# Up projection of an attention and feed-forward block: bias rows in two bands of 32 partitions, both halves of a tile issued together

## The reference, cut to what matters

```
q, k, v = split(x @ Wqkv.T + bqkv)            # 16 heads of 16
q, k = elu(q*scale) + 1, elu(k*scale) + 1
y = q * cumsum(k*v) / max(sum_d(q * cumsum(k)), 1e-3)
x = layernorm(x + y @ Wproj.T + bproj)
h = gelu(quant(x) @ quant(w_fc).T + b_fc)      # 256 -> 1024: the up projection
x = layernorm(x + quant(h) @ quant(w_proj).T + b_proj)   # 1024 -> 256: the down projection
```

## Time and profile before

| | us |
|---|---|
| median of 3 runs | 276.52 |
| lowest, highest | 276.45, 277.63 |
| span of the profiled execution, first to last instruction | 273.3 |
| busy: PE, DVE, POOL, ACT | 240.0, 238.9, 155.0, 151.0 |
| one middle stage, from one `mean_var_1` to the next | 29.6 |
| mean granted clock of TensorE, as a share of 2.4 GHz | 0.982 |

### The profile page before, as it was taken

How to read it: one execution, slowest core, us unless ns; L and a number is a source line. 1 busy time by engine, 2 the same in 40 slices (tenths; PEclk the granted TensorE clock), 3 DMA queues, 4 the chain that set the end, 5 groups by cost and what they waited for, 6 DMA issues and landing times.

```text
span 273.3 us, 3668 instructions
## 1 busy us (share of the span) xinstructions
PE 240.0 (88%) x1204; PEld 143.4 (52%) x1204; DVE 238.9 (87%) x513; ACT 151.0 (55%) x246; POOL 155.0 (57%) x118
## 2 busy tenths in 40 slices
PE   7999889997999899989999899989999989838761
PEld 7546636653566446644656356644664455524340
DVE  1398997998998999899989999899989997978962
ACT  2663277745556851855475754685285646332823
POOL 1076466575376656476566737675647656655851
PEclk9999999999999999999999999999999997979997
DMA  6940020036202473227304490238224530642022
GB/s 155 365 97 2 0 78 1 2 70 155 46 0 38 77 193 42 38 39 190 81 0 77 114 160 0 41 64 205 38 36 44 110 83 0 65 90 78 0 79 77
DMA packets 49474, 20.70 MB, mean 76 GB/s; under 512 B 38960, under 2 KB 49200, under 8 KB 49456
## 3 DMA queue, kind: packets, MB, share of 16 engines
q1 hardware_dynamic: 47824, 20.20, 32.7%
q10 hardware_dynamic: 1632, 0.27, 0.6%
HBM read 7.35 MB, written 4.19 MB: 42 GB/s over the span
## 4 chain that ended last, share of the span: by engine, by line
DVE 56%; PE 25%; DMA 8%; POOL 4%; issue 3%; ACT 2%; SPq 1%; ACTq 0%; POOLq 0%; DVEq 0%
DVE vbank L857 12%; PE abank L1116 8%; DVE hq L758 7%; DVE vbank L821 6%; PE dbank L1193 5%; DVE kvsum L799 4%; DMA h<-in_L_ffn_w_fc_dram 4%; POOL h_round L380 3%; PE hbank L1184 3%; DVE r L815 3%; DVE r L869 3%; DVE vbank L834 3%; DMA xqT<-xq 2%; DVE h_pow L750 2%; DVE kf L782 2%
## 5 line engine op out<-in xcount | busy, mean ns | idle before, releaser
L1116 PE MATMUL abank<-xT,WqkvT 128*128 128x512 f32 x176 | 81.6, 599 | 3.6 <-DVE kf L782 2.2
L380 POOL TENSOR_TENSOR h_round<-h,h_inv 128x1024 f16<-128x1024 f32 x32 | 66.5, 2079 | 31.2 <-DVE h_inv L753 28.5
L527 ACT ACTIVATE h<-hbank 128x512 f32<-128x512 f32 x64 | 36.7, 595 | 51.3 <-PE hbank L1184 51.0
L1116 PEld LDWEIGHTS abank<-xT,WqkvT 128*128 128x128 f32 x176 | 31.1, 190 | 36.2 <-issue 23.7
L857 DVE TENSOR_REDUCE vbank<-h 128x32 f32<-128x1024 f32 x32 | 39.1, 1221 | 1.6 <-ACT h L527 1.5
L349 POOL TENSOR_TENSOR qk<-qf,ksum 128x512 f32<-128x512 f32 x16 | 23.5, 1469 | 29.4 <-DVE ksum L794 18.6
L1184 PE MATMUL hbank<-w_fcT,xqT 128*128 128x512 bf16 x128 | 39.1, 387 | 0.0
L521 ACT ACTIVATE expz<-abank,zbias_neg 128x512 f32<-128x512 f32 x30 | 20.6, 687 | 31.9 <-PE abank L1116 31.4
L1193 PE MATMUL dbank<-w_prT,hT 128*128 128x256 bf16 x256 | 34.4, 279 | 1.9 <-DMA hT<-hq 1.3
L1148 PE MATMUL bbank<-WprojT,y 128*128 128x256 f32 x128 | 32.0, 380 | 0.0
L1193 PEld LDWEIGHTS dbank<-w_prT,hT 128*128 128x128 bf16 x256 | 25.2, 100 | 9.5 <-issue 3.3
(11 more groups left out here) (102 smaller groups left out, 357.4 us busy)
## 6 DMA issues: line engine op xcount, KB each, us to landing
x_sb<-in_L_attn_x_dram SPq DMA_DIRECT2D x8, 512.0 KB, 3.9
out_dram<-o_sb SPq DMA_DIRECT2D x7, 512.0 KB, 3.5
h<-in_L_ffn_w_fc_dram SPq DMA_DIRECT2D x1, 1024.0 KB, 9.6
h<-in_L_ffn_w_proj_dram SPq DMA_DIRECT2D x1, 1024.0 KB, 11.1
Wqkv_sb<-in_L_attn_Wqkv_dram SPq DMA_DIRECT2D x3, 256.0 KB, 6.3
out_dram<-o_sb SPq DMA_DIRECT2D x4, 128.0 KB, 1.7
hT<-hq SPq DMA_TRANSPOSE x28, 3.1
Wproj_sb<-in_L_attn_Wproj_dram ACTq DMA_DIRECT2D x1, 256.0 KB, 7.2
```

The source lines that it names most:

```text
L380: nc.gpsimd.tensor_tensor(h_round[:, t % 2].rearrange("p (g j) -> p g j", j=BLOCK_K), h[:, t].rearrange("p (g j) -> p g j", j=BLOCK_K), h_ ...
L527: nc.scalar.activation(h[:, t, half * HALF:(half + 1) * HALF], hbank[half][:, :], ACT.Gelu).then_inc(s_h, 1)
L1116: last = nc.tensor.matmul(ps[:, :], WqkvT[:, k, e * P:(e + 1) * P], xT[:, k], start=(k == 0), stop=(k == CC - 1))
```

## The change

The bias row parts of half 0 stay in partitions 0 to 2, those of half 1 go to partitions 32 to 34. The two bias matmuls of a tile contract over 32 partitions each, 0 to 31 and 32 to 63, stand next to each other and write to different banks. The two halves of a tile are one call `up(n, t)`, with one wait for both GELUs of the tile before, and with the order: bias 0, bias 1, two products of half 0, two products of half 1. Loading the bias rows takes 12 small DMAs where it took 9.

```diff
+    BAND = 32
...
-                    sp.dma_start(bias_rows[r:r + 1, 0:HID], b_part[:, r, 0:HC]).then_inc(s_brow, 16)
+                    sp.dma_start(bias_rows[r:r + 1, 0:HALF], b_part[0:P // 2, r, 0:HC]).then_inc(s_brow, 16)
+                    sp.dma_start(bias_rows[BAND + r:BAND + r + 1, HALF:HID], b_part[P // 2:, r, 0:HC]).then_inc(s_brow, 16)
...
-            def up(n, t, half):
-                if isinstance(n, int) and n == 0:
-                    pe.wait_ge(s_w16, 2)
-                    pe.wait_ge(s_brow, 9 * 16)
+            def up(n, t):
+                if isinstance(n, int) and n == 0 and t == 0:
+                    pe.wait_ge(s_w16, 4)
+                    pe.wait_ge(s_brow, 12 * 16)
                 wait(pe, s_xqT, 16 * n + (32 if n == CHUNKS - 1 and t >= 2 else 16))
-                cols = slice(half * HALF, (half + 1) * HALF)
-                nc.tensor.matmul(hbank[half][:, :], ones_k[:, :], bias_rows[:, cols], start=True, stop=False)
-                for c in range(CC):
-                    last = nc.tensor.matmul(hbank[half][:, :], xqT[:, t, c], w_fcT[:, c, cols],
-                                            start=False, stop=(c == CC - 1))
-                last.then_inc(s_h_ps, 1)
+                wait(pe, s_h, 8 * n + 2 * t)
+                for half in range(2):
+                    band = slice(BAND * half, BAND * (half + 1))
+                    nc.tensor.matmul(hbank[half][:, :], ones_k[band, :], bias_rows[band, half * HALF:(half + 1) * HALF], start=True, stop=False)
+                for half in range(2):
+                    for c in range(CC):
+                        last = nc.tensor.matmul(hbank[half][:, :], xqT[:, t, c], w_fcT[:, c, half * HALF:(half + 1) * HALF],
+                                                start=False, stop=(c == CC - 1))
+                    last.then_inc(s_h_ps, 1)
...
             def step(s):
...
                 n = s + 1
-                up(n, 0, 0)
                 n = s + 2
                 denominators(n)
                 n = s + 1
-                up(n, 0, 1)
-                wait(pe, s_h, 8 * n + 1)
-                up(n, 1, 0)
-                wait(pe, s_h, 8 * n + 2)
-                up(n, 1, 1)
+                up(n, 0)
+                up(n, 1)
                 n = s + 2
                 transpose_rec(n, 0)
                 transpose_rec(n, 1)
                 n = s + 1
-                wait(pe, s_h, 8 * n + 3)
-                up(n, 2, 0)
-                wait(pe, s_h, 8 * n + 4)
-                up(n, 2, 1)
+                up(n, 2)
                 n = s + 2
                 project_out(n, 0)
                 n = s + 1
-                wait(pe, s_h, 8 * n + 5)
-                up(n, 3, 0)
                 n = s + 2
                 project_out(n, 1)
                 n = s + 1
-                wait(pe, s_h, 8 * n + 6)
-                up(n, 3, 1)
+                up(n, 3)
                 n = s + 3
                 project(n, 1, 0, abank[0])
```

More of the change, by code:

```diff
@@ L1261, in _ @@
             transpose_x(2, 0, 0, abank[0])
[L1262 removed]
             denominators(1)
[L1264 to L1267 removed]
+            up(0, 0)
             pe.wait_ge(s_kv, 4)
             transpose_x(2, 0, 1, abank[1])
[L1270 to L1271 removed]
+            up(0, 1)
             transpose_rec(1, 0)
[L1273 to L1274 removed]
             transpose_rec(1, 1)
[L1276 to L1279 removed]
+            up(0, 2)
             project_out(1, 0)
[L1281 to L1282 removed]
+            up(0, 3)
             project_out(1, 1)
@@ L1369, in _ @@
             transpose_x(7, 1, 1, abank[1])
-            up(5, 0, 0)
             denominators(6)
-            up(5, 0, 1)
-            pe.wait_ge(s_h, 41)
-            up(5, 1, 0)
-            pe.wait_ge(s_h, 42)
-            up(5, 1, 1)
+            up(5, 0)
+            up(5, 1)
             transpose_rec(6, 0)
             transpose_rec(6, 1)
-            pe.wait_ge(s_h, 43)
-            up(5, 2, 0)
-            pe.wait_ge(s_h, 44)
-            up(5, 2, 1)
+            up(5, 2)
             project_out(6, 0)
-            pe.wait_ge(s_h, 45)
-            up(5, 3, 0)
             project_out(6, 1)
-            pe.wait_ge(s_h, 46)
-            up(5, 3, 1)
+            up(5, 3)
             project(7, 1, 0, abank[0])
@@ L1405, in _ @@
             down(5, 3)
-            up(6, 0, 0)
             denominators(7)
-            up(6, 0, 1)
-            pe.wait_ge(s_h, 49)
-            up(6, 1, 0)
-            pe.wait_ge(s_h, 50)
-            up(6, 1, 1)
+            up(6, 0)
+            up(6, 1)
             transpose_rec(7, 0)
             transpose_rec(7, 1)
-            pe.wait_ge(s_h, 51)
-            up(6, 2, 0)
-            pe.wait_ge(s_h, 52)
-            up(6, 2, 1)
+            up(6, 2)
             project_out(7, 0)
-            pe.wait_ge(s_h, 53)
-            up(6, 3, 0)
             project_out(7, 1)
-            pe.wait_ge(s_h, 54)
-            up(6, 3, 1)
+            up(6, 3)
             down(6, 0)
@@ L1432, in _ @@
             transpose_xq_half(7, 0)
-            up(7, 0, 0)
-            up(7, 0, 1)
-            pe.wait_ge(s_h, 57)
-            up(7, 1, 0)
+            up(7, 0)
             transpose_xq_half(7, 1)
-            pe.wait_ge(s_h, 58)
-            up(7, 1, 1)
-            pe.wait_ge(s_h, 59)
-            up(7, 2, 0)
-            pe.wait_ge(s_h, 60)
-            up(7, 2, 1)
-            pe.wait_ge(s_h, 61)
-            up(7, 3, 0)
-            pe.wait_ge(s_h, 62)
-            up(7, 3, 1)
+            up(7, 1)
+            up(7, 2)
+            up(7, 3)
             transpose_hq(7, 0)
```

17 lines of the change are left out of this document (1 added, 16 removed).

## The result

The changed kernel takes 298.63 us, median of 4 runs (297.05 to 300.57), against 276.82 us (276.45 to 277.63) for the kernel before on the same chip. The ratio is 1.0775, 95% interval 1.0714 to 1.0837: 22 us slower, where 1.5 were forecast and the range ended at 281.5. The profiled execution took 299.99 us, with a span of 297.7.

A forecast was written before the change was run, and what follows sets the result against it. DVE was taken to bound the middle stages, so a shorter PE gains nothing. Terms 0.8 - 0.15 (chunk 2) + 0.7 + 0.15 = +1.5 us gave 278.0 us against 276.52, range 277.2 to 278.8 (overall 276.0 to 281.5).

The forecast's parts named there:

- What is hidden: Delays in middle stages, loading and last chunk said to be covered by waits or slack elsewhere: no cost.
- The bound: Middle stages: DVE bounds them, its instructions nearly gapless; a shorter PE is worth nothing there.
- Rival 4: Whole kernel: PE is on the path and pays at its 25% chain share, 1.7 us, time 274.8; chance 0.10.
- The pair's cost, 0.22: PE's queue: two bias matmuls run side by side in one slot, 0.22 us; alternatives 0.43 unshared, 0.75 drained.
- Rival 1: Bias pairs: not side by side, or array drains; 279.7 us, with full drain up to 285.2; chance 0.17.
- PE busy falls by about 7: Sign to look for on PE: its busy time drops by about 7 us with the pairs side by side.
- Tile 0 behind `denominators`, +0.2 a stage: Stages of chunks 1, 3, 4, 5: h of tile 0 comes later, 0.2 us each, +0.8 in all.
- the exponential: Middle stages, fourth tile: `project` 0.7 us late, but 1.1 of cover before `feature` reads the exponential, so no cost.
- +0.7 for chunk 6: Stage of chunk 6, low clock: five slots instead of three behind `denominators`, h of tile 0 0.87 later; +0.7 us.
- +0.15 for chunk 0: Chunk 0, fourth tile: both halves start together, the second GELU ends later than DVE wants it; +0.15 us.
- The last chunk: End of program: h of tile 0 some 0.1 us earlier, of tile 1 some 0.1 later; no cost.
- rival 2: Middle stages: PE's clock falls more often from waits beside small `denominators`; 1.2 us per stage, 279.2 to 284; chance 0.14.

The follow-up runs named there:

- e5: Kernel before without the 64 bias matmuls of the up projection (h lacks its bias): 277.65 us, ratio 1.0003.
- e11: Changed kernel with both halves' bias rows in partitions 0 to 2 and both bias matmuls over partitions 0 to 31, the same array rows: 307.72 us, ratio 1.1075.
- e13: Kernel before with an overwritten matmul of 8 columns over 32 partitions added ahead of each half's full height bias matmul: 280.04 us, ratio 1.0101.
- e3: Changed kernel with unread full height filler matmuls, three ahead of `denominators` and four behind tile 0, in chunks 0 to 6: 283.88 us, ratio 1.0227.
- e1: Changed kernel with its new order, but both bias matmuls over all 128 partitions: 285.99 us, ratio 1.0313.
- e12: e1 with the same filler matmuls as e3: 283.76 us, ratio 1.0223.
- e2: Kernel before in its old order, each bias matmul over 32 partitions, never side by side: 289.4 us, ratio 1.0351.
- e10: Kernel before in its old order, bias matmuls of the up projection over 64 partitions: 289.23 us, ratio 1.0424.
- e7: e1 with both halves of tile 0 moved ahead of `denominators`: 279.04 us, ratio 1.0065.
- e4: Changed kernel with both halves of tile 0, pair included, moved ahead of `denominators`: 289.1 us, ratio 1.0412.
- e9: Kernel before in its old order, bias matmuls of the up projection over 96 partitions: 278.77 us, ratio 1.0018.
- e6: Changed kernel with bands of 64 partitions, so a pair covers all 128 between its two matmuls: 293.31 us, ratio 1.0527.
- e14: Kernel before with an overwritten matmul of 8 columns over all 128 partitions added ahead of each half's bias matmul: 277.57 us, ratio 0.9987.

## Why the prediction was wrong

The step that failed first by size is the clock: the forecast held it at 1.00 in the middle stages and put its fall at nothing, leaving it to a rival. It was 0.89 to 0.95 there, and the low matmuls cost 12.6 us by it. The second is "What is hidden", with the tail: the order was summed at 1.5 us and cost 9.2. The parts one by one:

**The bound** was read rightly. e5 takes 10.2 us off PE and the time does not move; DVE bounds the middle. Rival 4 (PE on the path, 274.8) is out, as it wanted a quarter of the saving.

**The pair's cost, 0.22.** The bands run side by side (e11), and there is a gap of a tenth behind each pair and ahead of some: the cost is 0.32 to 0.42. In the forecast side by side and a gap stood as alternatives, 0.22 or 0.75, where they add. Rival 1's bound for the gaps, 0.16 on each side, was the right kind of row and 1.6 times too wide. The forecast's "PE busy falls by about 7" was never to be had. The Trainium skill has tiles of different row groups running at once in "TensorE: Matmul & The Clock Gate", Part 3, Packing small matmuls: the trace agrees (e11). The Trainium skill also has a change of tiling mode draining the array in "TensorEngine Tiling (Array Packing)", Key Properties: the gaps agree (0.19 there and back in e13), though none is seen ahead of the pair behind the transposes (e3).

**Tile 0 behind `denominators`, +0.2 a stage.** With the pair at 0.42 the same sum gives 0.4, and L859 waits 0.38 in the changed kernel and 0.39 in e1, whose two serial slots are as long. The sum was right in its form and short by the pair. There is some luck in it: in e1 `denominators` starts 0.05 behind `qk` (137.55 for 137.50) and not 0.17, and takes 1.81 and not 1.70 (to 139.36), and the two errors cancel.

**"What is hidden": the exponential.** This step failed. It gave `project` a delay of 0.7 and set it against a cover of 1.1, from the end of an exponential at 122.17 to its reader at 123.29. In e1, with the pair at two slots, `feature` waits 0.34 and the stage of the earlier trace rows is 0.9 longer. The prediction had this case, but only at 0.75 for the pair, where it gave 0.7 under rival 1. By its own sum two slots delay `project` by 0.7 + 2 x 0.21 = 1.1, just the cover, so the pair's size is one part of the error and some 0.3 of cover that was not there is the other.

**The tail and the head.** The forecast held +0.7 for chunk 6 and +0.15 for chunk 0. e1 is 1.0 late at the first stage and 4.0 longer in the tail, at a clock of 0.88 for 0.92. The last chunk was put at "nothing"; in the changed kernel its four L859 each wait for a GELU, by 0.9 to 1.5 us, with PE at the low clock:

```profile
273.30 1.23 DVE L859 TENSOR_REDUCE vbank<-h 128x32 f32<-128x1024 f32 x1 [1.09 <-ACT h L529]
...
282.91 1.23 DVE L859 TENSOR_REDUCE vbank<-h 128x32 f32<-128x1024 f32 x1 [1.50 <-ACT h L529]
```

All of the order together is 9.2 us (e1 less before) where 1.5 were summed; 2.2 of it go with the filler (e12).

**The clock: rival 2, at 0.14, is what happened**, and it was wrong in cause and in size. Its cause was PE's wait next to the small `denominators`. The runs show that this pattern alone does nothing in the middle (e1 has it, at 1.00), and that low matmuls bring the clock down without it (e2, e10). Where both meet the height costs 12.6 us, for 10 with tile 0 first (e7 to e4) and 3.5% in the old order (e2); full height filler in the idle places takes the loss away (e3), so PE's idle time, or the want of full height work in it, has a part too. Its size was 1.2 us a stage, from one short low stretch; the stretches last 3.4 and 6.8 us, past the slack of PE's queue (29.56 - 27.60 = 1.96 us a stage), and the tail's clock of 0.66 was not in the case at all.

The 22 us (276.8 to 298.6) divide, by medians, into 9.2 for the order, of which 7.0 hang on tile 0's place, and 12.6 for the height, all of it clock (e3 against e12). The medians of the kernel before lay from 276.7 to 277.8 between groups, so each part is good to about a microsecond. The saving is small twice over: the gaps at the switch eat most of it on PE (0.32 to 0.42 for 0.43, some 0.2 us a stage at full clock), and in the old order PE had next to nothing to give (e5).

Three things stay open. Why e7 gains 7.0 us on e1, where its stages are 0.45 shorter: in the profiled executions, which lie only 3.6 apart, 3.3 of it is in the tail (69.6 to 66.3 us), but no run holds the tail's clock alone. The step between 96 and 64 partitions was not divided further. And whether low columns without the gaps around them would let the clock fall was not tried.

## What to carry to other kernels

Before packing small matmuls, take them out altogether in one run: if the time does not move, as here, there is next to nothing for the packing to win. A low pair between full height matmuls pays up to two gaps of a tenth of a microsecond, so a pair of 512 columns saved 0.01 to 0.11 us of the 0.21 hoped for; and in this kernel it took the clock down with it, which made PE the bound and cost more than all else. When two bounds on a cost come from different causes, ask whether both can hold: here they added up.

## What the runs showed of the hardware that was not expected

- Matmuls of 512 columns over 32 or 64 partitions, in this kernel's queue, let TensorE's granted clock fall from 1.00 to 0.50 for microseconds at a time while PE was busy throughout (e10, windows above). Over 96 partitions they hardly did: 1.00 from 90 to 210 in e9, and 0.94 from 60 to 90, as in e7 with full height alone.
- Two low matmuls side by side that cover all 128 partitions between them do not prevent it (e6: 293.3 us, clock 0.89 to 0.95 in four of five middle stages).
- Low matmuls of 8 columns at the same places leave the clock at 1.00 (e13).
- A switch between a low and a full height matmul costs about 0.10 us each way (0.19 there and back, e13 against e14). Behind eight transposes, or a wait, the gap ahead of the low pair is not seen (e3: 1.00 for 1.00 of e12).
- More work made the kernel faster: seven full height matmuls added to a stage took 14.7 us off the changed kernel (e3).
